# Cross attention through per-head products of value and output weights, with packed probabilities, in a two-block transformer kernel

## The reference

```
q = (x @ wq); k = (ctx @ wk); v = (ctx @ wv)          # per head, ctx is 77 x 128
attn = softmax(q k^T / sqrt(64))                      # per head, 128 x 77
out = (attn @ v, heads side by side, 128 x 1024) @ wo + bo
```

## Time and profile before

| | before |
|---|---|
| median of 3 runs | 942.78 us |
| the profiled execution, from first to last instruction | 942.8 us |
| PE, weight loads, DVE, ACT, POOL busy | 803.7, 673.0, 568.8, 540.2, 360.0 us |
| mean granted TensorE clock | 0.909 |
| stage 1 (attention, feed forward) | 0 to about 538 us |

### The profile page before, as it was taken

One profiled execution on the slowest core, in us unless ns is written; L12 is line 12 of the kernel. 1 busy time (PEld: TensorE's weight loads), 2 busy tenths in 40 slices (PEclk: granted clock), 3 DMA queues, 4 the chain that ended last, 5 costly groups with the idle time before them and its releaser, 6 DMA issues.

```text
span 942.8 us, 18988 instructions
## 1 busy us (share of the span) xinstructions
PE 803.7 (85%) x6173; PEld 673.0 (71%) x6173; DVE 568.8 (60%) x1941; ACT 540.2 (57%) x1147; POOL 360.0 (38%) x559
## 2 busy tenths in 40 slices
PE   5899899999999999999987588999978786861693
PEld 5777787888878888788876456999746565651693
DVE  2576887677866668776575352333558787885012
ACT  2565676667766677666754222333448888851362
POOL 1233454333333333332656150566422222226363
PEclk9897999999999999999998789999855979795697
DMA  9699111001010101000100131888600000001574
GB/s 284 230 314 342 70 37 37 15 1 50 2 37 1 51 1 37 15 1 37 48 27 20 45 105 40 245 249 243 209 7 1 1 0 1 1 1 37 152 208 126
DMA packets 43275, 78.50 MB, mean 83 GB/s; under 512 B 5339, under 2 KB 28587, under 8 KB 42651
## 3 DMA queue, kind: packets, MB, share of 16 engines
q1 hardware_dynamic: 39691, 70.09, 23.8%
q0 software_dynamic: 3488, 7.20, 2.2%
HBM read 63.98 MB, written 30.13 MB: 100 GB/s over the span
## 4 chain that ended last, share of the span: by engine, by line
PE 55%; DVE 20%; issue 9%; POOL 6%; ACT 6%; DMA 2%; SPq 2%; DVEq 0%; ACTq 0%; POOLq 0%
PE bank L899 5%; PE bank L627 5%; PE bank L689 5%; PE bank L652 4%; PE bank L642 3%; DVE sb_smax L1396 3%; PE bank L633 3%; PE bank L677 3%; DVE sb_row_sum L1406 3%; PE bank L907 3%; PE bank L661 3%; PE bank L1008 2%; PE bank L1016 2%; DVE sb_st_all L1704 2%; PE bank L718 2%
## 5 line engine op out<-in xcount | busy, mean ns | idle before, releaser
L1881 POOL TENSOR_TENSOR sb_expd<-sb_expd,sb_rden 128x512 f32<-128x512 f32 (+1 forms) x128 | 112.4, 878 | 259.4 <-DVE sb_rden L1410 259.3
L1396 DVE TENSOR_REDUCE sb_smax<-bank 128x4 f32<-128x512 f32 (+1 forms) x128 | 74.1, 579 | 64.3 <-PE bank L652 39.7
L1973 POOL TENSOR_TENSOR sb_rstd_all<-sb_rsq_all,sb_halves 128x4 f32<-128x4 f32 x44 | 45.2, 1026 | 133.5 <-DVE sb_rsq_all L1711 133.5
L677 PE MATMUL bank<-sb_eye,sb_expd 128*128 128x128 f32 (+1 forms) x512 | 77.5, 278 | 5.7 <-POOL sb_expd L1881 5.2
L1118 ACT ACTIVATE sb_expd<-sb_shifted 128x512 f32<-128x512 f32 (+1 forms) x128 | 69.8, 545 | 18.9 <-DVE sb_shifted L1399 17.9
L677 PEld LDWEIGHTS bank<-sb_eye,sb_expd 128*128 128x128 f32 (+1 forms) x512 | 59.7, 145 | 26.8 <-issue 13.5
L1406 DVE TENSOR_REDUCE sb_row_sum<-sb_expd 128x4 f32<-128x512 f32 (+1 forms) x128 | 73.0, 570 | 9.4 <-ACT sb_expd L1118 9.4
L1112 ACT ACTIVATE sb_probT<-bank 128x512 f32<-128x512 f32 (+1 forms) x128 | 74.3, 590 | 7.2 <-PE bank L677 6.9
L1399 DVE TENSOR_TENSOR sb_shifted<-bank,sb_smax 128x512 f32<-128x512 f32 (+1 forms) x128 | 75.0, 586 | 4.4
L627 PE MATMUL bank<-sb_h1T,sb_watt 128*128 128x128 f32 x512 | 72.1, 287 | 4.7 <-DMA sb_watt<-att_w 2.3
L689 PE MATMUL bank<-sb_probT,sb_v 128*64 128x128 f32 (+1 forms) x1024 | 71.7, 283 | 5.0 <-issue 3.4
(11 more groups left out here) (256 smaller groups left out, 1917.2 us busy)
## 6 DMA issues: line engine op xcount, KB each, us to landing
sb_up_w<-gate_up SPq DMA_DIRECT2D x38, 384.0 KB
rows_b<-pad_b SPq DMA_DIRECT2D x1, 8775.0 KB, 53.6
rows_a<-pad_a SPq DMA_DIRECT2D x1, 7670.0 KB, 27.9
sb_up_w<-w1b SPq DMA_DIRECT2D x23, 256.0 KB
sb_v<-v_all SPq DMA_DIRECT2D x16, 308.0 KB
v_all<-sb_v_rows SPq DMA_DIRECT2D x9, 512.0 KB, 2.6
sb_blk_x<-rows_a SPq DMA_DIRECT2D x38, 65.0 KB, 3.3
sb_watt<-att_w SPq DMA_DIRECT2D x4, 512.0 KB, 6.3
```

Of the source, the lines that this page charges most:

```text
L677: mm = pe.transpose(trans[u % 2][0:n, h, :], expd[:, (units_before(i) + u) % EXP_RING, h, 0:n], eye[:, :])
L1396: dve.tensor_reduce(smax[:, u % 2, :], s_in, X, ALU.max).then_inc(max_done, 1)
L1881: pool.tensor_tensor(e, e, rden[:, u % 2, :].unsqueeze(2).broadcast_to([P, QH, n]), ALU.mult).then_inc(norm_done, 1)
```

## The change

**Weights multiplied per head.** In iteration 0 PE makes B2 = wv (head h) times wo (head h), 128 x 128 for each of 16 heads ("b2_0" to "b2_3"). The context's block is now multiplied with B2, 2048 columns in four products ("v2_0" to "v2_3"), so that the output product is folded in. The blocks are made one iteration later than before, since B2 exists only behind iteration 0. `v2_rows` still holds 1024 columns: the block is stored in two halves, the second from the same buffer once the first has been stored.

**Packed probabilities.** ACT writes the exponentials of all 16 heads side by side (16 x 77 = 1232 columns, `expd2`); PE turns them in ten tiles of 128 columns instead of sixteen of 77, and "wo2" becomes ten accumulated products of the turned tiles with the stored values (`cross_out`). The cross attention's `pv_pair`, the copies of its outputs and its `o_proj` are gone. In DRAM the values lie by sequence, head and row, 512 bytes each; a block is stored in pieces by sequence.

**Order.** "zT" now stands ahead of "v1_0", and "logit" behind it. The first loads: context and the two weights of "a2" directly behind the first attention weights, the rest of x later, the new products' weights last. The empty rows are filled in 8 parts, one pair of DMAs in each of iterations 1 to 8. `gact` is gone; the gelu works in place.

The core of the diff:

```diff
-    (("v1_1",), ()),
-    (("wo1",), ("g2_2", "ffout")),
-    ((), ("hT",)),
-    ((), ("v1_0", "zT")),
-    (("logit",), ()),
+    (("v1_1",), ("b2_0",)),
+    (("wo1", "b2_1"), ("g2_2", "ffout")),
+    (("v2_2",), ("hT", "b2_2")),
+    (("b2_3",), ("v2_3",)),
+    (("zT", "v1_0"), ("logit",)),
...
-V2_BLOCK = {i: v2_blocks(i) - 1 for i in range(B) if v2_blocks(i) > v2_blocks(i - 1)}
+V2_BLOCK = {i + 1: v2_blocks(i) - 1 for i in range(B) if v2_blocks(i) > v2_blocks(i - 1)}
+
+def v2_pieces(n):
+    found, last = [], min(P * (n + 1), B * C)
+    for b in range(P * n // C, -(-last // C)):
+        first, end = max(P * n, C * b), min(last, C * (b + 1))
+        found.append((b, first - C * b, end - C * b, first - P * n, end - P * n))
+    return found
...
             def store_values(i):
                 n = V2_BLOCK[i]
-                last = min(P, B * C - P * n)
-                sp.wait_ge(emptied["act"], max(PLAN[i, "v2_0"][2], PLAN[i, "v2_1"][2]))
-                sp.dma_start(v2_all[P * n:P * n + last, :], v2_rows[0:last, :]).then_inc(v2_stored, 16)
+                by_batch = v2_all.rearrange("(b h k) d -> b k h d", h=H, k=C)
+                for half in range(2):
+                    sp.wait_ge(emptied["act"], max(PLAN[i, f"v2_{2 * half + j}"][2] for j in range(2)))
+                    for b, k0, k1, p0, p1 in v2_pieces(n):
+                        sp.dma_start(by_batch[b, k0:k1, 8 * half:8 * half + 8, :],
+                                     v2_rows[p0:p1, :].rearrange("p (h d) -> p h d", h=8)).then_inc(v2_stored, 16)
 
             def load_values(b):
-                sp.wait_ge(v2_stored, 16 * v2_blocks(b))
+                sp.wait_ge(v2_stored, 16 * v2_stores(v2_blocks(b)))
                 if b >= 2:
-                    sp.wait_ge(pv_done, units_before(b) // 2)
-                sp.dma_start(v2[:, b % 2, :, :].rearrange("c h d -> c (h d)"),
-                             v2_all[C * b:C * (b + 1), :]).then_inc(v2_in[b % 2], 16)
+                    sp.wait_ge(proj_full, PLAN[b, "wo2"][1])
+                whole, first = CHUNKS - 1, H * C * b
+                sp.dma_start(v2[:, b % 2, 0:whole, :],
+                             v2_all[first:first + whole * P, :].rearrange("(c p) d -> p c d", p=P)).then_inc(v2_in[b % 2], 16)
+                sp.dma_start(v2[0:H * C - whole * P, b % 2, whole, :],
+                             v2_all[first + whole * P:first + H * C, :]).then_inc(v2_in[b % 2], 16)
 
             def values(i):
                 if i in V2_BLOCK:
                     store_values(i)
-                load_values(i)
...
+                load_values(i - 1)
...
+            for i in range(1, B + 1):
                 values(i)
+                if i <= PAD_PARTS:
+                    empty_rows(i - 1)
...
+            def cross_out(i, name):
+
+                t = use(i, name)
+                for c in range(CHUNKS):
+                    k = min(P, H * C - P * c)
+                    mm = pe.matmul(t[:, 0:D], probT2[0:k, c, :], v2[0:k, i % 2, c, :], start=(c == 0), stop=(c == CHUNKS - 1))
                 mm.then_inc(proj_full, 1)
...
                 if name == "wo2":
-                    pe.wait_ge(o_kept, at(i, lambda t: units_before(t) // 2))
-                    o_proj(i, name, "B", wo[1])
+                    pe.wait_ge(probT_ready, units_before(i))
+                    pe.wait_ge(v2_in[i % 2], 32 * (i // 2))
+                    cross_out(i, name)
...
+                    if name == "v2_0":
+                        from_one(act, v2_stored, 16 * v2_stores(n))
+                    if name == "v2_2":
+                        act.wait_ge(v2_stored, 16 * (v2_stores(n) + len(v2_pieces(n))))
```

More of the change, by code:

```diff
@@ L61 @@
     (("lin",), ()),
-    (("v1_1",), ()),
-    (("wo1",), ("g2_2", "ffout")),
-    ((), ("hT",)),
-    ((), ("v1_0", "zT")),
-    (("logit",), ()),
-]
+    (("v1_1",), ("b2_0",)),
[3 more added lines that the diff above has]
+    (("zT", "v1_0"), ("logit",)),
+]
+CHUNKS = -(-H * C // P)
+HEAD_END = [QH * C * (j + 1) // P if j + 1 < QH else CHUNKS for j in range(QH)]
+UNIT_CHUNKS = [range(HEAD_END[j - 1] if j else 0, HEAD_END[j]) for j in range(QH)]
 AT = {"wo2": 2, "gate": 5, "gelu": 6, "glu": 6, "sums": 9, "logit": 10, "exp": 5, "rank": 2}
-STREAM = {n: s for s, names in (("A", "wo1"), ("B", "a2_0 a2_1 a2_2 a2_3 g2_0 g2_1 g2_2 g2_3 g2_4 g2_5 h2T v2_0 v2_1"),
+STREAM = {n: s for s, names in (("A", "wo1"), ("B", "a2_0 a2_1 a2_2 a2_3 b2_0 b2_1 b2_2 b2_3 g2_0 g2_1 g2_2 g2_3 g2_4 g2_5 h2T v2_0 v2_1 v2_2 v2_3"),
                                 ("C", "wo2 h3T gate lin ffout zT logit"),
@@ L155, in present @@
 def present(i, name):
-    if name[:2] == "a2":
+    if name[:2] in ("a2", "b2"):
         return i == 0
@@ L173, in v2_blocks, with v2_stores @@
     return -(-C * (b + 1) // P)
-V2_BLOCK = {i: v2_blocks(i) - 1 for i in range(B) if v2_blocks(i) > v2_blocks(i - 1)}
+V2_BLOCK = {i + 1: v2_blocks(i) - 1 for i in range(B) if v2_blocks(i) > v2_blocks(i - 1)}
[5 more added lines that the diff above has]
+    return found
+def v2_stores(n):
+    return 2 * sum(len(v2_pieces(m)) for m in range(n))
 def proj_plan():
@@ L198, in units_before, with pairs_before @@
     return sum(QH * (("A" in streams(j)) + ("B" in streams(j))) for j in range(-1, i))
+def pairs_before(i):
+    return sum(QH // 2 for j in range(-1, i) if "A" in streams(j))
 def units(S, steps):
@@ L711, in fill @@
                         mm = pe.matmul(t[:, h * P:(h + 1) * P], qk2_w[p, 1, c, :], qk2_w[p, 0, c, :], start=True, stop=True)
+                    mm.then_inc(proj_full, 1)
+                if name.startswith("b2"):
+                    if name == "b2_0":
+                        pe.wait_ge(ld_vo2, 32)
+                    t, j = use(i, name), int(name[-1])
+                    p = slice(DH * (j % 2), DH * (j % 2) + DH)
+                    for h in range(QH):
+                        c = 4 * (j // 2) + h
+                        mm = pe.matmul(t[:, h * P:(h + 1) * P], vo2_w[p, 0, c, :], vo2_w[p, 1, c, :], start=True, stop=True)
                     mm.then_inc(proj_full, 1)
@@ L721, in fill @@
                 if name.startswith("v2"):
-                    if i == 0:
-                        pe.wait_ge(ld_att2, 64)
+                    if i == 1:
+                        emptied_by(0, "b2_3")
                     rows_ = slice(P * V2_BLOCK[i], min(P * V2_BLOCK[i] + P, B * C))
-                    v_proj(i, name, wv[1], ctxT[:, rows_], half, rows_.stop - rows_.start)
+                    v_proj(i, name, b2, ctxT[:, rows_], int(name[-1]), rows_.stop - rows_.start)
                 if name.startswith("q1"):
@@ L730, in fill @@
                 if name.startswith("v1"):
-                    v_proj(i, name, wv[0], h1T[:, i + 1, :], half, P)
+                    v_proj(i, name, wv, h1T[:, i + 1, :], half, P)
                 if name == "wo1":
@@ L1073, in fill @@
                     last = min(P, B * C - P * n)
-                    if n and name == last_of(i, "v2", first=True):
-                        act.wait_ge(v2_stored, 16 * n)
-                    empty(i, name, v2_rows[0:last, half * 512:(half + 1) * 512], lambda t: t[0:last, :])
+                    if name == "v2_0":
+                        from_one(act, v2_stored, 16 * v2_stores(n))
+                    if name == "v2_2":
+                        act.wait_ge(v2_stored, 16 * (v2_stores(n) + len(v2_pieces(n))))
+                    empty(i, name, v2_rows[0:last, half % 2 * 512:(half % 2 + 1) * 512], lambda t: t[0:last, :])
                 if name == "hT":
```

144 lines of the change are left out of this document (80 added, 64 removed).

## The result

| | before | after |
|---|---|---|
| median of 4 runs, us | 942.76 (941.45 to 943.51) | 1048.22 (1046.76 to 1053.13) |
| span of the profiled execution | 942.8 | 1044.9 |
| mean granted clock | 0.909 | 0.870 |

What follows compares the result with a forecast made beforehand. PE's queue of work was taken to bound the first stage. The terms: 942.8 - 2.5 + 1.3 + 4 - 2.5 + 74.5 + 19 = 1036.6, lowered to 1032 us for overlap; range 980 to 1060.

Steps and rivals of the forecast that it cites:

- The new wait: PE ahead of "wo2", ten times, for values stored and loaded back: 74.5 us in all, longest 14.5 in iteration 10.
- the prediction's formula: Values ready at F + 3.2 + 0.2 + 1.5 + store + 3.6, F ending "ffout", against when "wo2" is due.
- the load: Values' way back from memory ahead of "wo2": 1.5 fixed plus 75 pieces at 0.0276, 3.6 us each time.
- The store: Second half of a block going to memory: 0.2 and 1.5 us each, plus 53.2 over ten blocks for moving pieces.
- the unevenness: Stores use the largest engine count up to 16 dividing the rows: 53.2 us over ten blocks, 17.7 if even.
- rival 2: Even stores: the round trip is exposed but spreads well, waits 39 us, shorter half-clock stretches (15), 997 us; chance 0.22.
- The clock: PE at half clock behind each of the ten waits: 1.9 us lost each, 19 us in all.
- The stretch behind a gap in front of zC: Iterations without a block (3, 6, 8, 11, 13): if the clock falls, 1.7 us each; half counted, +4.
- How much of PE's work comes through: First stage: PE's work falls by 15.5 us, but the zC chain leaves only about 2.5 us as time.
- 942.8 - 2.5 + 1.3 + 4 - 2.5: Span before, tail gain, a "v2_0"/"v2_1" pair moved from iteration 0, clock in iterations without a block, start gain.
- The start: First loads and iteration 0: PE gets about 5 us ahead, "v2_1" gives 1, B2 takes 4.2: -2.5 (0 to -5).
- The last step: From 1036.6 to 1032: waits swallow some of the 4 us, and some half-clock time falls into them.

Runs made afterwards that it cites:

- e3: The changed kernel with each stored piece cut at the largest multiple of 16 rows; 1032.99 us, ratio 1.094 to the kernel before.
- e1: The changed kernel with the values for "wo2" loaded from a constant input, copies and stores still made; 1030.58 us, ratio 1.092 to the kernel before.
- e2: The changed kernel with each block from sequence 2 on made an iteration earlier, SP's order the same; 1022.45 us, ratio 1.084 to the kernel before.
- e5: e2 with each load issued right behind its own block's store, a whole iteration ahead of use; ratio 1.034 to the kernel before, 975 at 942.8.
- e12: e5 with "v2_0" in step 3, but blocks 0 and 1 made in steps 0, 2, 6, 7; ratio 0.997 to the kernel before, 940 at 942.8.
- e8: e4 with the empty rows written in eight pieces behind the value loads of iterations 1 to 8; ratio 0.989 to the kernel before, 932 at 942.8.
- e4: The kernel before with only its first loads reordered: context and four cross attention weights first, rest of x last; 935.81 us, ratio 0.991.
- e10: e5 with all copies of a block made earlier and each store cut at a multiple of 16 rows; ratio 1.018 to the kernel before.

## Why the prediction was right

**The new wait.** Ten times, behind the blocks foreseen, the longest in iteration 10. By the prediction's formula and by PE's timeline, in us:

```
iteration      2    3    5    6    8   10   11   13   15   16   sum
forecast     7.0  5.2  6.3  5.3  5.2 14.5  5.4  9.1 10.7  5.9  74.5
measured     8.4  6.9  6.6  6.7  5.8 14.0  6.6 10.0 10.7  6.4  82.1
```

The sum is 7.6 us larger. The term that was mis-sized is the load: 3.6 us in the forecast, and from the load's issue to the product 4.5 to 5.2 by the timelines, 46.5 in sum where 36 was reckoned. The load is two transfers, the second issued 0.4 us behind the first, and both need 4.3 us at the median (KB each, median us to landing, in the DMA view of after's whole execution):

```profile
sb_v<-v_all SPq DMA_DIRECT2D x16, 576.0 KB, 4.3
...
sb_v<-v_all SPq DMA_DIRECT2D x16, 40.0 KB, 4.3
```

The store went the other way: from its issue to the load's, 66.1 us in sum where 70.2 was reckoned (ten times 0.2 and 1.5, and 53.2), since a lone engine took 24 ns a piece and not 27.6. That is why block 5's wait alone came out below its forecast, and why the sum of all ten looks better than its terms: 10.5 too little and 4.1 too much; the 1.2 left lie at the two ends. Store and load together came out 6.4 us longer, where the Trainium skill's fixed cost of about 2 us would have put on 10, by the prediction's estimate. That figure ("DMA: Bandwidth & Descriptors", section "Anatomy of one DMA — SWDGE (gpsimd) path") is a fit for DMAs issued by GpSimd; SP issues the ones here, and no run separates their fixed part from the moving one.

e3 confirms the unevenness (rival 2 with even stores from the start would have been 997). It took 19.7 us off the store's part, where the forecast's own terms had 35.5 (53.2 against 17.7); the 16.7 us that its additional issues take make up that difference.

**What the step left out.** The forecast followed the wait through landing and load only. e1 and e2 show that SP's order holds the load even with no landing to wait for, and e5 that both must go. That changes nothing in the number, since the two run over the same stretch; it would have misled whoever mended the kernel by the prediction alone.

**The clock.** Forecast: 19 us behind the waits. In the ten stretches with a mean of 0.52 to 0.65 that begin inside the waits, some 48 us of PE's work ran at half clock, as in the stretch of 374.00 above with 4.22 us: about 24 us lost, half of it each time. That is 5 us more than said: three stretches last 13.7 us rather than 3.4 to 4, though over half of each lies in the wait itself. The stretch behind a gap in front of zC was forecast at +4 in sum, with half of five; all five came, 3.4 us each, 8.5 lost.

**One wait that wasn't foreseen.** In iteration 2 "v2_2" wants a bank that VectorE still reads:

```profile
117.15 1.70 PE L679 MATMUL bank<-sb_watt,sb_ctxT 128*128 128x512 f32 x2 [3.65 <-DVE sb_xa L1460]
```

**How much of PE's work comes through.** The forecast had 15.5 us less work and only 2.5 us of it as time, because the chain to zC takes 3.22 us anyway. This is the step that the experiments bear out best. Iteration 7, without a block, in before and in e5:

```profile
234.20:263.00 28.80, 28.07 (x252) 23.76 (x251) 21.82 (x65) 19.54 (x35) 10.96 (x16) 1.00 0.03 10
```

```profile
253.70:281.90 28.20, 25.76 (x217) 21.80 (x215) 21.80 (x65) 17.75 (x33) 10.96 (x16) 1.00 0.58 207
```

2.3 us of work less, 0.6 us of time less. With all waits gone, the forecast's own terms give 942.8 - 2.5 + 1.3 + 4 - 2.5 = 943.1; e12 is 940. And against e8, which has the loads and the empty rows but not the new cross attention, e12's last iteration starts 7.5 us later (502.2 against 494.7), the 0.8% between their ratios: 2.0 at the start, for B2, 3.1 in iteration 2, and the rest in small differences of the other iterations.

**The start.** -2.5 was forecast; in after iteration 1 starts at 47.9 instead of 49.9, and PE has no DMA wait at "a2". The order alone is worth more, 5.2 us at that point in e4, and B2 takes the difference back. What was missed is that the reordering also saves half clock in iteration 1: all of that stretch in e4, most of it in after, where the iteration takes 30.6 us instead of 32.7.

**The sum.** The terms added up to 1036.6, and the median is 11.6 us higher. Those named above are 7.6 in the waits, 5 in the clock behind them, 4.5 behind zC's gaps and 3.7 at the bank, 20.8 in all. Against them, iteration 1 was 2.1 us shorter than before and the rest of the kernel, behind this stage, some 5 us; about 2 us stay unassigned. The last step, from 1036.6 down to 1032 because half-clock time would fall into the waits, went the wrong way: the clock's terms came out larger, not smaller.

## What to carry to other kernels

A value that goes through memory and back costs its landing, its place in the queue that issues the load, and the one buffer that it leaves from; each of the three hid the next. Taking away the landing alone moved the time by 2 to 3% (e1, e2), where all together moved it by 11%. Ask of every load not only when its data is ready, but what stands ahead of it in its queue. Work taken from the busiest engine is time only where no chain through the other engines spans the same stretch: here 2.3 us of work gave 0.6.

## What was not expected of the hardware

- One uneven store holds up more than itself. In after's trace SP's issue of block 5's two pieces took 8.19 us (a median issue takes 0.36):

```profile
L551 SPq DMA_DIRECT2D v_all<-sb_v_rows x50: 218/362/8097, 60.1 to 600.8; - x50
```

  (duration in ns: lowest, median, highest). The 8 us are the issue of the 75 rows behind the 53, in both halves of the block, and again in both halves in e12; in e3 and e10, with the stores cut, no store's issue takes over 1.7 us. So with 424 pieces in one engine's list the next transfer isn't even issued at once, and all that stands behind it on SP waits as well. In e1 the load itself is held so, 7.10 us behind block 8. It is not a matter of uneven stores alone: the 80-row part of a load that stands behind two empty-row transfers took 4.7 to 5.1 us to issue in after (at 130.55, 238.16 and 305.19). What bounds the issue no run shows.
- What a wait costs in clock grew with it: with the waits of 10 to 14 us (iterations 10, 13, 15) the clock was at the lower of its two levels, 1.2 GHz, for 13.7 us, and with most of those of 6 to 7 us for 6.8 us. Each of these stretches begins inside the wait, so that only its end costs work. In iterations 5 and 13 of after (granted clock is the third number from the end):

```profile
199.90:206.70 6.80, 3.41 (x17) 3.44 (x18) 0.86 (x2) 0.83 (x2) 1.04 (x1) 0.53 1.06 379
...
486.70:500.40 13.70, 6.25 (x37) 5.93 (x37) 0.49 (x3) 0.32 (x1) 1.04 (x1) 0.52 0.36 96
```
